# A three-layer graph attention block: products, scores, exponentials and residuals put in another order, and the turn of the normed tokens behind down product 6

## The chip, the cores and the metric

The kernel runs on one core of a Trainium2 chip. The metric is the device time of one execution in microseconds, lower is better. A core has five engines with a queue each: TensorE (PE: matrix products and transposes, results in PSUM), VectorE (DVE), ScalarE (ACT: activations), GpSimd (POOL), and SyncE (SP), which here issues all DMAs. The queues run in order and meet through semaphores.

## The reference

Sixteen graphs of 512 tokens with 256 features, and an adjacency matrix each. All is in fp32.

```python
h = maximum(layernorm(x), 0)
for l in range(3):                                    # the L0 network
    scores = si[:, :, None] + sj[:, None, :] + attn_b[l]   # si, sj = h @ attn_w[l, :256], h @ attn_w[l, 256:]
    attn = softmax(where(adj or diagonal, leaky_0.2(scores), -inf), axis=-1)
    y = layernorm(h + attn @ h) * g1[l] + beta1[l]
    h = layernorm(y + gelu(y @ W1[l] + b1[l]) @ W2[l] + b2[l]) * g2[l] + beta2[l]
x = x + h
h = maximum(layernorm(x), 0)
Wh = h @ W                                            # the L1 network, W is 256 x 256
e = where(adj > 0, leaky_0.2(Wh @ a1 + (Wh @ a2).T), -9e15)
x = x + leaky_0.2(softmax(e, axis=1) @ Wh)
```

## The kernel before

**Pairs and slots.** The graphs are worked in eight pairs. For a pair there are six slots, one per layer and side (a side is one graph of the pair). Slot n does the feed-forward of layer l for the graph of its side, and beside it the attention of the other graph (step n + 1), which will have its feed-forward in the next slot. `Slot` (line 241) says what else falls into a slot. With k = 2 x layer + side, and not in the first pair: in k = 0 and k = 2 a graph of the pair before enters the L1 network (`s.final`: normalise, turn, project, bounded scores), and one slot later, in k = 1 and k = 3, its output is made (`s.late`: exponentials, column scale, product, leaky residual, store). In k = 4 and 5 the next pair's input and masks are prepared (`s.prepare`). Where the attention step is one of layer 0 (`soon`; k = 5 and k = 0) the scores come from the input and are there early.

**Precision.** The feed-forward products are made in three fp32r passes: high x high, high x low, low x high. So h (transposed, normed tokens) and the gelu outputs each exist as a high part and a low part. `h_split` (line 687, ScalarE) makes of the turned tokens in PSUM `h_hi[k]` and `h_full[k]` for k = 0, 1; `h_rest` (line 946, VectorE) makes `h_lo[k]` from `h_full[k]`. `gelu` (line 695, ScalarE) makes the full value `g_full` and the high part `gelu_hi`; `gelu_rest` makes `gelu_lo`, on VectorE for f = 1, 3, 4 and on GpSimd for f = 0, 2, 5, 6, 7. `gelu_hi` and `gelu_lo` are rings of three.

**TensorE's order in a slot.** `up_first` (both first output blocks of W1), `up` 2 and 3, `down` 0 and 1, then `up` and `down` alternating, with the other graph's work between: `scores_row` (s_j as a row for the neighbour maximum), `bound_rows`, `attend_out` (the attention product), and at the end of the slot `turn_tokens` (transposes of `normed` into `ps_t`), `down` 6 and `down` 7. Each `down` adds into `acc`; the first one, line 473, also adds the residual by a transposing product (`residual`, line 466).

**VectorE's order in a slot.** `ff_norm` of the graph before (line 963): statistics of `acc` (L970), variance, high part of gelu 0 (L956), dot products for the next scores (L983), shifts (L992), gelu_lo 1 (L960), then from the dots s_i and s_j (L1006, L1011, L1015); `neighbour_max` (line 875), gelu_lo 3 and 4, `bounded_scores`, `attention_sum`, `attention_norm` (L942), `prepare_masks` where due, and `h_rest`; in slots with `s.final`, `final_bounded` (line 1045) with `h_rest` in it. GpSimd makes the inverse roots (L1236), gelu_lo (L1270), the scaled layer input (L1246, L1250), half of the masked scores (L1276) and the low part of the weights in the first pair (L1291). An order written out by hand, no planner, sets all of this.

The tail of a slot on TensorE before:

```python
                up(n, layer, 7)
                down(n, side, layer, 5)
                pe.wait_ge(q_ready.sem, q_ready.at(n + 1))
                turn_tokens(normed, ln1_apply, h_tr, n + 1, ps_t)
                down(n, side, layer, 6)
                if s.prepare is not None:
                    mask_transposes(s.prepare, side, free)
                down(n, side, layer, 7)
```

On GpSimd, `gelu_rest(n, 7)` stands behind a wait for all four chunks of `ln1_apply` (lines 1330 to 1333). On ScalarE, a change between exponentials and gelus is a table load (ACT_TABLE_LOAD).

## Time and profile before

| | |
|---|---|
| median of 3 runs | 2128.69 us (2128.28 to 2129.1) |
| the profiled execution | 2126.3 us, span 2124.5 us |
| busy: TensorE products, weight loads | 1907.7 us (90%), 1618.6 (76%) |
| busy: VectorE, ScalarE, GpSimd | 1637.2 (77%), 1254.6 (59%), 880.9 (41%) |
| mean granted TensorE clock | 0.969 of full |
| DMA | 52.34 MB, mean 25 GB/s |

The profile is of one execution; times in its rows count from the start of the span. The end of a TensorE product is modelled, and products overlap, so two products that follow each other start closer than their durations. The granted clock has two levels here, 1.2 and 2.4 GHz; a mean of 0.96 in a stretch says that part of it ran at the lower one.

### The profile page before, as it was taken

What the parts mean: (1) busy time and instruction counts of PE and PEld (TensorE: products, weight loads), DVE (VectorE), ACT (ScalarE), POOL (GpSimd) and SP (SyncE); (2) the same over time, 40 slices, a digit from 0 to 9 for tenths busy, and PEclk for the clock granted to TensorE, in tenths of its full rate; (3) what the DMA queues carried; (4) which work ended last, traced back from release to release, by engine and by line L of the source; (5) the groups of instructions that cost most, each with busy time, mean ns of one, the idle gap of its engine ahead of it and who ended that gap; (6) DMA issues with size and microseconds to landing.
All of it is one profiled execution on the core that took longest, in us unless ns stands there. A gap on an engine that the chain in (4) does not pass through costs nothing.

```text
span 2124.5 us, 30899 instructions
## 1 busy us (share of the span) xinstructions
PE 1907.7 (90%) x11009; PEld 1618.6 (76%) x11009; DVE 1637.2 (77%) x4980; ACT 1254.6 (59%) x1948; POOL 880.9 (41%) x703
## 2 busy tenths in 40 slices
PE   3888899998998989999899998999899898999995
PEld 2777777787787877778778777777787787777874
DVE  6778887688777887878878688777886678876765
ACT  3555566566666565665665655656556666565662
POOL 2345453335433444333534344433443334533351
PEclk9999999999999999999999999999999999999998
DMA  4000100010000110001100001000100011000100
GB/s 159 21 30 21 60 11 21 1 40 31 11 21 1 40 41 1 21 1 41 40 1 21 11 35 35 1 21 21 50 11 15 7 39 32 11 11 1 31 1 20
DMA packets 40626, 52.34 MB, mean 25 GB/s; under 512 B 2926, under 2 KB 30872, under 8 KB 40472
## 3 DMA queue, kind: packets, MB, share of 16 engines
q1 hardware_dynamic: 40472, 50.37, 7.3%
q8 instruction: 87, 1.43, 0.3%
q14 instruction: 67, 0.55, 0.1%
HBM read 41.97 MB, written 8.39 MB: 24 GB/s over the span
## 4 chain that ended last, share of the span: by engine, by line
PE 42%; DVE 35%; POOL 9%; ACT 8%; issue 7%; DMA 0%; DVEq 0%; POOLq 0%; ACTq 0%
PE acc L423 11%; PE acc L489 9%; PE ps_u L462 7%; PE acc L526 5%; DVE probs L910 4%; POOL columns L1236 4%; PE acc L508 3%; PE ps_t L386 2%; POOL probs L1276 2%; DVE junk L983 2%; DVE probs L1049 2%; DVE columns L992 2%; DVE junk L881 2%; DVE probs L1053 2%; DVE stats L970 2%
## 5 line engine op out<-in xcount | busy, mean ns | idle before, releaser
L489 PE MATMUL acc<-w_hi,gelu_hi 128*128 128x256 f32 x1536 | 475.7, 310 | 0.0
L702 ACT ACTIVATE g_full<-ps_u,vec_all 128x512 f32<-128x512 f32 x384 | 259.1, 687 | 348.8 <-PE ps_u L462 186.6
L1270 POOL TENSOR_TENSOR gelu_lo<-g_full,gelu_hi 128x512 fp32r<-128x512 f32 x240 | 312.9, 1308 | 320.9 <-ACT gelu_hi L710 260.6
L489 PE MATMUL acc<-w_lo,gelu_hi 128*128 128x256 f32 x1536 | 437.7, 285 | 0.0
L489 PE MATMUL acc<-w_hi,gelu_lo 128*128 128x256 f32 x1536 | 437.5, 285 | 0.0
L423 PE MATMUL acc<-x_nat,probs 128*128 128x257 f32 x1536 | 374.8, 393 | 34.1 <-ACT probs L677 22.8
L423 PEld LDWEIGHTS acc<-x_nat,probs 128*128 128x128 f32 x1536 | 279.4, 191 | 127.2 <-ACT probs L677 42.9
L1236 POOL TENSOR_TENSOR columns<-columns 128x4 f32<-128x4 f32 x128 | 136.0, 1063 | 533.2 <-DVE columns L842 533.2
L489 PEld LDWEIGHTS acc<-w_hi,gelu_hi 128*128 128x128 f32 x1536 | 298.7, 194 | 4.9
L489 PEld LDWEIGHTS acc<-w_lo,gelu_hi 128*128 128x128 f32 x1536 | 298.5, 194 | 5.1
L489 PEld LDWEIGHTS acc<-w_hi,gelu_lo 128*128 128x128 f32 x1536 | 295.9, 193 | 0.0
L462 PE MATMUL ps_u<-h_hi,w_hi 128*128 128x512 f32 x576 | 244.4, 424 | 32.9 <-ACT g_full L702 26.3
L1276 POOL TENSOR_TENSOR probs<-probs,mask_t 128x512 f32<-128x512 f32 x96 | 130.2, 1359 | 339.8 <-DVE probs L910 335.2
L462 PE MATMUL ps_u<-h_hi,w_lo 128*128 128x512 f32 x576 | 234.0, 406 | 0.0
L462 PE MATMUL ps_u<-h_lo,w_hi 128*128 128x512 f32 x576 | 233.9, 406 | 0.0
L710 ACT ACTIVATE gelu_hi<-ps_u,vec_all 128x512 fp32r<-128x512 f32 x336 | 230.5, 686 | 0.0
L910 DVE SCALAR_TENSOR_TENSOR probs<-ps_t,columns,low_sb 128x512 f32<-128x512 f32 x192 | 135.0, 745 | 99.4 <-ACT low_sb L672 94.3
L462 PEld LDWEIGHTS ps_u<-h_hi,w_hi 128*128 128x128 f32 x576 | 112.5, 195 | 70.3 <-issue 40.3
L677 ACT ACTIVATE probs<-probs,columns 128x512 f32<-128x512 f32 x192 | 129.7, 718 | 46.5 <-POOL probs L1276 46.4
L526 PE MATMUL acc<-wh,probs 128*128 128x256 f32 x512 | 120.5, 390 | 14.2 <-DVE wh L1085 14.2
L462 PEld LDWEIGHTS ps_u<-h_hi,w_lo 128*128 128x128 f32 x576 | 112.8, 196 | 26.5
L462 PEld LDWEIGHTS ps_u<-h_lo,w_hi 128*128 128x128 f32 x576 | 113.2, 197 | 15.7
(129 smaller groups left out, 3703.3 us busy)
## 6 DMA issues: line engine op xcount, KB each, us to landing
adj_in<-adj_dram SPq DMA_DIRECT2D x64, 256.0 KB, 2.7
x_nat<-x_dram SPq DMA_DIRECT2D x16, 512.0 KB, 5.2
x_res<-x_dram SPq DMA_DIRECT2D x16, 512.0 KB, 4.2
out_dram<-x_res SPq DMA_DIRECT2D x64, 128.0 KB, 1.7
x_res<-L_gnn_W_dram SPq DMA_DIRECT2D x5, 1024.0 KB, 5.6
mask_g<-L_gnn_W_dram SPq DMA_DIRECT2D x1, 1024.0 KB, 12.3
attn_row<-L_gnn_attn_w_dram SPq DMA_DIRECT2D x1, 512.0 KB
g_row<-L_gnn_g_dram SPq DMA_DIRECT2D x1, 384.0 KB
```

Source lines behind the costliest of these rows:

```text
L423: last = pe.matmul(acc[side][c % 2][:, 0:D + 1], probs[:, j, c * P:(c + 1) * P], x_nat[:, side, j, :], start=(j == 0), stop=(j == NC - 1))
L462: last = pe.matmul(ps_u[f % 2][:, :], w[:, layer, k, lhs], h[:, k, :], start=(i == 0), stop=(i == len(terms) - 1))
L489: last = pe.matmul(acc[side][c // 2][:, cols:cols + D], h[:, r, tok], w[:, layer, f, :], start=False, stop=(f == FC - 1 and i == 2), skip_ ...
L508: last = pe.matmul(banks[c % 2][:, 0:D + 2], h_last[:, k, c * P:(c + 1) * P], w_last[:, k, :], start=(k == 0), stop=(k == KC - 1))
L526: last = pe.matmul(banks[c % 2][:, 0:D], probs[:, j, c * P:(c + 1) * P], wh[:, j, 0:D], start=(j == 0), stop=(j == NC - 1))
L677: act.activation(probs[:, j, :], probs[:, j, :], ACT.Exp, bias=s_j2[:, j:j + 1]).then_inc(p_ready.sem, 1)
L702: full = act.activation(g_full[:, f % 2, :], ps_u[f % 2][:, :], ACT.Gelu, bias=b1_col[:, layer, f:f + 1])
L710: act.activation(gelu_hi[:, f % RING, :], ps_u[f % 2][:, :], ACT.Gelu, bias=b1_col[:, layer, f:f + 1]).then_inc(gelu_done.sem, 1)
L910: dve.scalar_tensor_tensor(out=probs[:, j, :], in0=ps_t[1][:, :], scalar=s_j8[:, j:j + 1], in1=low_sb[:, :], op0=ALU.add, op1=ALU.max).the ...
L1236: pool.tensor_tensor(to[:, :], var_eps[:, :], minus_half[:, :], ALU.pow).then_inc(done.sem, 1)
L1270: pool.tensor_tensor(gelu_lo[:, f % RING, :], g_full[:, f % 2, :], gelu_hi[:, f % RING, :].bitcast(F32), ALU.subtract).then_inc(lo_done[0] ...
L1276: pool.tensor_tensor(probs[:, j, :], probs[:, j, :], mask_t[:, side, j, :], ALU.add).then_inc(q_masked[0].sem, 1)
```

## The change

It touches the order of work on all four compute engines, and the making of the scores:

- **Turn.** `down` 6 is issued before the turn of the normed tokens, not behind it.
- **h.** `h_split` makes `h_hi[0]`, `h_hi[1]`, then `h_full[0]`, `h_full[1]`. In `final_bounded`, `h_rest` stands after the second greatest value (j == 1), not behind the loop.
- **Scores.** The mean of each attention vector is taken off the vector in the setup of the first pair (8 setup steps per layer for 6), so that the dot products need no correction by the token's mean; both constants are summed into one, which `neighbour_max` adds to s_i. Three waits and four instructions behind the dots become one multiplication. The scaling of s_j moves behind the row chain, with a semaphore (`sj_scaled`) that `bounded_scores` waits for.
- **Late slots** (k = 1, 3). `final_exps` of chunks 0 and 1 moves from the end of the slot before to behind gelu 1; gelu 2 and its low part move behind `ff_apply` and `layer_input`; both `final_scale` move behind the scores; `final_out` of chunks 0 and 1 and `scores_row` move in front of `up` 4.
- **Residual.** Where the slot is not `soon`, `residual` of chunk 0 is issued in front of `up` 2.
- **Others.** gelu 6 before `input_apply` and `keep_mask` on ScalarE; gelu_lo 5 and 6 before `residual_shift` on GpSimd; `final_mask` of k = 5 behind `neighbour_max`.

```diff
@@ down, start_of, slot (TensorE)
-                        residual(n, side, c)
+                        if c not in turned:
+                            residual(n, side, c)
...
-                if s.attend and s.layer_a == 0 and not s.begins:
+                soon = s.attend and s.layer_a == 0 and not s.begins
+                if soon:
                     scores_row(n + 1)
+                else:
+                    residual(n, side, 0)
...
                 down(n, side, layer, 1)
-                if s.attend and s.late is None and (s.layer_a > 0 or s.begins):
+                if s.late is not None:
+                    final_out(s.late[0], acc[s.other], (0, 1), n - 1)
+                if s.attend and (s.layer_a > 0 or s.begins):
                     scores_row(n + 1)
                 up(n, layer, 4)
...
-                if s.late is not None:
-                    final_out(s.late[0], free, (0, 1), n - 1)
-                if s.late is not None:
-                    scores_row(n + 1)
                     final_out(s.late[0], free, (2, 3))
...
                 down(n, side, layer, 5)
+                down(n, side, layer, 6)
 
                 pe.wait_ge(q_ready.sem, q_ready.at(n + 1))
                 turn_tokens(normed, ln1_apply, h_tr, n + 1, ps_t)
-                down(n, side, layer, 6)
@@ h_split and the slot (ScalarE)
                                    bias=beta1_col[:, layer, k:k + 1], scale=g1_col[:, layer, k:k + 1]).then_inc(hi_ready.sem, 1)
+                for k in range(KC):
                     act.activation(h_full[:, k, :], ps_t[k][:, :], ACT.Identity, bias=both_col[:, layer, k:k + 1],
...
-                    gelu(n, layer, 2)
+                    if s.late is None:
+                        gelu(n, layer, 2)
+                    else:
+                        final_exps(s.late[0], (0, 1))
...
                         ff_apply(n - 1, other, 1)
+                    if s.late is not None:
+                        gelu(n, layer, 2)
...
                     gelu(n, layer, 5)
+                    gelu(n, layer, 6)
...
-                    gelu(n, layer, 6)
...
-                    if s.final is not None:
-                        final_exps(s.final[0], (0, 1))
@@ neighbour_max, ff_norm, final_bounded (VectorE)
-                dve.tensor_scalar(s_j8[:, :], s_j, 1.0 - SLOPE, None, ALU.mult)
-                dve.tensor_scalar(s_j2[:, :], s_j, SLOPE, None, ALU.mult)
+                if layer > 0:
+                    dve.tensor_scalar(s_i, s_i, bias_col[:, 0, layer:layer + 1], None, ALU.add)
                 dve.wait_ge(sj_bc.sem, sj_bc.at(n))
...
+                dve.tensor_scalar(s_j8[:, :], s_j, 1.0 - SLOPE, None, ALU.mult)
+                dve.tensor_scalar(s_j2[:, :], s_j, SLOPE, None, ALU.mult).then_inc(sj_scaled.sem, 1)
...
-                if late is not None:
-                    final_scale(late, 0)
...
-                if late is not None:
-                    final_scale(late, 1)
...
-                    for t in (1, 0):
-                        last = dve.scalar_tensor_tensor(out=raw_dots[:, t, :], in0=mean[:, :],
-                                                        scalar=minus_sum[:, t, layer:layer + 1],
-                                                        in1=raw_dots[:, t, :], op0=ALU.mult, op1=ALU.add)
...
-                    dve.tensor_tensor(raw_dots[:, :, :], raw_dots[:, :, :],
+                    dve.tensor_tensor(s_both[:, :, :], raw_dots[:, :, :],
                                       rstd[:, :].rearrange("p (o c) -> p o c", o=1).broadcast_to([P, 2, NC]),
-                                      ALU.mult).then_inc(dots_ready.sem, 1)
-                    dve.wait_ge(dots_ready.sem, dots_ready.at(turn, 2))
-                    dve.tensor_tensor(s_both[:, :, :], raw_dots[:, :, :],
-                                      bias_col[:, :, layer:layer + 1].broadcast_to([P, 2, NC]),
-                                      ALU.add).then_inc(s_ready.sem, 1)
+                                      ALU.mult).then_inc(s_ready.sem, 1)
                     dve.wait_ge(s_ready.sem, s_ready.at(step_next))
+                if late is not None:
+                    final_scale(late, 0)
+                    final_scale(late, 1)
...
-                if step is not None:
-                    h_rest(*step)
+                    if step is not None and j == 1:
+                        h_rest(*step)
@@ the slot (VectorE and GpSimd)
-                    if s.side == 1 and s.layer == LAST:
-                        final_mask(pair * 2 + 1, 1)
-                    neighbour_max(n + 1, other)
+                    neighbour_max(n + 1, other, s.layer_a)
...
                         if s.prepare is not None and s.side == 1:
+                            final_mask(pair * 2 + 1, 1)
                             prepare_masks(s.prepare, 1, (0,))
...
-                    gelu_rest(n, 2)
+                    if s.late is None:
+                        gelu_rest(n, 2)
...
+                    if s.late is not None:
+                        gelu_rest(n, 2)
...
+                    gelu_rest(n, 5)
+                    gelu_rest(n, 6)
                     if s.layer == LAST:
                         residual_shift(pair, s.side)
-                    gelu_rest(n, 5)
-                    gelu_rest(n, 6)
```

## Rows read from the trace of the kernel before

**Rows 1.** The page, section 1: busy time (share of the span) x instructions.
```profile
PE 1907.7 (90%) x11009; PEld 1618.6 (76%) x11009; DVE 1637.2 (77%) x4980; ACT 1254.6 (59%) x1948; POOL 880.9 (41%) x703
```

**Rows 2.** Windows: stretch, length; busy us (instructions) per engine; clock; DMA; GB/s.
```profile
52.84:301.14 248.30, 218.49 (x1257) 186.21 (x1257) 201.27 (x572) 140.12 (x205) 117.64 (x84) 0.95 0.10 30
852.63:896.37 43.74, 41.28 (x238) 34.79 (x237) 33.92 (x114) 27.90 (x43) 17.10 (x14) 1.00 0.08 25
685.03:729.79 44.76, 42.59 (x238) 36.06 (x237) 35.73 (x116) 27.90 (x43) 16.33 (x13) 0.96 0.14 48
896.37:940.44 44.07, 40.59 (x234) 34.50 (x233) 31.11 (x90) 26.79 (x43) 15.95 (x13) 0.96 0.00 1
474.47:515.09 40.62, 35.00 (x222) 29.98 (x221) 35.33 (x109) 24.52 (x39) 19.66 (x16) 1.00 0.08 26
984.23:1027.70 43.47, 37.83 (x223) 32.91 (x221) 36.60 (x115) 25.31 (x40) 19.63 (x16) 0.92 0.11 35
1027.70:1066.75 39.05, 36.10 (x222) 31.68 (x221) 34.76 (x102) 23.07 (x38) 20.21 (x16) 0.96 0.05 17
```

**Rows 3.** Waits of TensorE: us in total, times, longest us.
```profile
PE ps_t L386 <- DVE s_both L1015: 34.7, 18, 2.0
PE ps_t L432 <- DVE normed L942: 27.8, 12, 3.1
PE ps_t L386 <- DVE columns L892: 21.5, 8, 3.3
```

**Rows 4.** Timeline, turn to next slot (1 to 2): start, us, instruction, [idle before].
```profile
892.65 1.03 PE L432 MATMUL ps_t<-ident,normed 128*128 128x128 f32 x8
...
895.62 0.78 ACT L692 ACTIVATE h_last<-ps_t,vec_all 128x512 f32<-128x512 f32 x1
...
896.43 0.75 DVE L949 SCALAR_TENSOR_TENSOR h_lo<-h_last,vec_all,h_hi 128x512 fp32r<-128x512 f32 x1 [0.51 <-ACT h_last L692]
```

**Rows 5.** Timeline, head of slot 2, which starts at 896.37.
```profile
897.22 1.43 DVE L970 BATCH_NORM_STATS2 stats<-acc 128x6 f32<-128x256 f32 x4
...
904.48 1.45 DVE L1006 SCALAR_TENSOR_TENSOR raw_dots<-columns,vec_all,raw_dots 128x4 f32<-128x4 f32 x2
...
907.19 1.18 DVE L1015 TENSOR_TENSOR s_both<-raw_dots,vec_all 128x8 f32<-128x8 f32 x1
...
904.51 1.28 POOL L1246 TENSOR_TENSOR x_nat<-normed,g_row 128x512 f32<-128x512 f32 x1
...
908.42 0.93 PE L386 MATMUL ps_t<-ident,s_both 128*128 128x128 f32 x4 [1.95 <-DVE s_both L1015]
```

**Rows 6.** Timeline, head of slot 1 (late), which starts at 852.63.
```profile
852.68 1.28 ACT L736 ACT_TABLE_LOAD   x1
...
853.90 1.40 DVE L949 SCALAR_TENSOR_TENSOR h_lo<-h_last,vec_all,h_hi 128x512 fp32r<-128x512 f32 x2
...
856.20 1.42 DVE L970 BATCH_NORM_STATS2 stats<-acc 128x6 f32<-128x256 f32 x4
...
868.31 0.17 DVE L1015 TENSOR_TENSOR s_both<-raw_dots,vec_all 128x8 f32<-128x8 f32 x1
...
857.64 0.47 PE L462 MATMUL ps_u<-h_hi,w_hi 128*128 128x512 f32 x1 [1.32 <-ACT g_full L702]
...
859.61 1.29 POOL L1270 TENSOR_TENSOR gelu_lo<-g_full,gelu_hi 128x512 fp32r<-128x512 f32 x1
```

**Rows 7.** Timeline, end of slot 4, which ends at 1027.70.
```profile
1017.98 0.16 DVE L842 SCALAR_TENSOR_TENSOR columns<-columns 128x4 f32<-128x4 f32 x1
...
1019.84 1.02 POOL L1236 TENSOR_TENSOR columns<-columns 128x4 f32<-128x4 f32 x1
...
1022.35 1.51 POOL L1270 TENSOR_TENSOR gelu_lo<-g_full,gelu_hi 128x512 fp32r<-128x512 f32 x1 [1.50 <-DVE normed L942]
...
1021.45 1.73 PE L432 MATMUL ps_t<-ident,normed 128*128 128x128 f32 x7 [2.53 <-DVE normed L942]
```

**Rows 8.** Timeline, bound rows of slot 5, which starts at 1027.70.
```profile
1041.65 1.67 PE L386 MATMUL ps_t<-ident,columns 128*128 128x128 f32 x7 [2.57 <-DVE columns L892]
```

29 lines of the change are left out of this document (15 added, 14 removed).

## The prediction

> **What bounds the kernel now.** I read the page's first two sections, then the windows view, then the waits of TensorE, then the timeline. TensorE is busy 90% of the span [rows 1], so the change, which takes no product away, can win at most the idle tenth and what the slow clock adds. I call the eight products of one feed-forward f = 0 to 7, and I number the six slots of a pair 0 to 5 (2 x layer + side); a slot starts with the first product of `up_first`. The windows view [rows 2] shows the first pair (248.30 us) and slots of later pairs, and where the clock falls: in one late slot of 44.76 us the mean is 0.96, in another of 43.74 it is 1.00; it is 0.96 in slots 2 and 5, 1.00 and 0.92 in two slots 4. The waits of TensorE [rows 3] name three large causes: the scores of the next layer (34.7 us, 18 times), the normed tokens of the turn (27.8 us, 12 times) and the bound rows (21.5 us, 8 times). These are waits for VectorE's chain, so the question of each part is what it does to VectorE's time within the slot.
>
> **Part 1, the turn behind down product 6, high parts first.** Today a turn starts at 892.65, ScalarE's last full part ends at 896.39, VectorE's last low part at 897.18, and the next slot starts at 896.37 [rows 4]. Turn and two down products fill the 3.72 us between; the turn, 1.03 with its overlap into the next product, fills some 0.85 of them, and half of the rest is 1.43 for one product. Moved in front, product 6 fills a wait of the turn where there is one. Where there is none (slots 0 to 3 of later pairs), the turn starts 1.43 later in a slot of the same length, so `h_rest` ends and the next `ff_norm` starts 1.43 later in the next slot: 2.3 after its start in place of 0.85 [rows 5]. TensorE itself hardly waits there: both high parts are now ready 1.5 after the first can be made, product 7 covers that, and the low parts come at most 0.3 late.
> What that delays: down product 0 waits for `gelu_lo` 0, which ends 4.7 us after `ff_norm` starts (856.20 to 860.90 in slot 1 [rows 6]). So in slots 2 and 4 product 0 starts at 6.95 of the slot, about 0.75 later than today; the wait is short and I expect no fall of the clock from it.
> In late slots (1 and 3) it is worse. `h_rest` now stands after the second of the bounded rows and waits there for ScalarE's third activation of the new order; the last bounded rows and maxima come behind it: 0.9 us from the end of `h_rest` (855.30) to `ff_norm` (856.20) today [rows 6], and the 1.3 that stood before it, together 2.2. `ff_norm` starts 4.5 into the slot, today 3.57 [rows 6], and `gelu_lo` 0 is done at 9.25 instead of 8.27. Taking the exponentials off ScalarE's head (a table load of 1.28 and two exponentials, for which up product 2 waits 1.32 [rows 6]) wins 0.9 at up product 2, but this is lost again, as product 0 waits for VectorE: one wait of 2.9 us. Behind a wait of 2.57 in slot 5 seven transposes take 1.67 us [rows 8], where eight of the turn take 1.03 [rows 4]: the clock has fallen. A mean of 0.96 over 44.07 us is 3.4 us at half pace, up to 1.7 lost; six of the 14 late slots lose 1.0 already (44.76 against 43.74 [rows 2]). So I add 0.85 on average for the clock. Fourteen late slots times (0.95 + 0.85) = **+25 us**; bounds +0.5 and +3.3 each, so +7 and +46.
>
> **Part 2, fewer steps to the scores.** Two L1006, one L1011 and one L1015 become one multiplication. In slot 2 they run from 904.48 to 908.37, and TensorE waits 1.95 us for them [rows 5]. L1015 takes 1.18 there and 0.17 in slot 1 [rows 6]; L1006 ends at 905.93, just behind POOL's first instruction of `layer_input` (904.51 to 905.79) [rows 5], and L1011 and L1015 behind the next two. So I count one such stall for the one instruction that is left. With `ff_norm` 1.43 later, and `gelu` 2 on ScalarE later by the same, the last shift ends at 9.65 of the slot, and the multiplication at 9.8 (not held) or 11.0 (held); TensorE arrives at 10.6. I take 11.0, today 12.05: 1.05 won.
> The Trainium skill, page "SBUF — State Buffer", section "Who interferes with whom", says that a DVE instruction with two SBUF inputs contends with a GpSimd instruction that reads SBUF, and that whoever comes first holds the pair for the whole instruction. By that rule the one multiplication left is held up and the gain is 1.05, by its absence 1.45; the trace agrees (1.18 against 0.17).
> In slot 2 everything behind is ScalarE's: final apply, two gelus, `final_h`, which set when `project` starts. So the whole win is what moves `final_shift`, 1.0 to 1.2: seven slots, **-7.7 us** (bounds -5 and -17). The scaling of s_j behind the row chain and the bias in front of it are two small instructions against two; the scaling is hidden by VectorE's wait for the bound rows. The early `residual` of token chunk 0, 0.22 us, falls into the 0.4 us that up product 2 waits; in slots 2 to 4 the later wait gives it back, so nothing.
>
> **Part 3, slot 4.** Here both things meet. The scores come 1.05 earlier and the slow stretch behind them (up to 1.5 us, in two of six such slots with both) goes. At the end, POOL makes the inverse root only at 1019.84 although the variance is ready at 1018.14, because gelu_lo 6 waited for ScalarE, which made `keep_mask` first; the turn waits 2.53 us [rows 7]. In the new order gelus 5 and 6 precede the input and the mask, so the root starts at once (1.7 earlier), and product 6 (1.43) covers what is left. What comes next: product 7 waits for `gelu_lo` 7, which POOL makes only behind the four normed chunks (1022.35 to 1023.86, 1.6 behind the chunks' end [rows 7]), and the mask's transposes wait for chunk 3 of `prepare_masks`, 1.9 behind it. That is a wait of 0.6. Counted through: slot 4 takes 37.5 us; the six of today take between 40.62 and 43.47, mean 42.2 [rows 2]. Six times -4.7 = **-28 us** (bounds -2.0 and -5.5 each).
>
> **Part 4, slots 5 and 0.** Slot 5 starts nearer to VectorE's mask, scores and `h_rest` of the slot before, so `ff_norm` starts at 2.9 of the slot, today 1.08: VectorE is the bound of slot 5 (34.76 of 39.05 us busy [rows 2]). `final_mask`, 1.13 us, leaves its place before the row chain, and the held scaling too; the bound rows then come at 13.2 to 14.4, today 13.95 [rows 8]. But mask and scaling are only put behind, before `bounded_scores`, and POOL's `layer_input` is still at work then; TensorE's attention product of chunks 2 and 3 waits for VectorE. I get +0.3 to +2.6, take +1.5: six slots **+9 us**. Slot 0 is 0.3 later each, seven times: **+2 us**. The last pair's slot 4 has no masks (-1.1), and the last slot runs on VectorE's chain (+1.2): nothing.
>
> **Part 5, the first pair.** It has no late slots and its turns wait most (3.1 us at the longest [rows 3]). Here the turn does not move later, so VectorE keeps its place in the slot and the scores are ready before TensorE comes: slots 1 and 2 win 2.0 us of wait and 1.5 of clock each, slot 3 some 2.0. But at the turn only about 0.3 is won, since product 7 then waits for `gelu_lo` 7 (product 6 used to cover that). With 5 from slot 4, 1.3 lost in slot 5, and four more setup steps in shadow: -0.3 -4.1 -4.0 -3.3 -5 +1.3 = **-15 us** (bounds -8 and -18).
>
> **Sum.** 25 - 7.7 - 28 + 9 + 2 - 15 = -15 us on the profiled execution of 2126.3 us (span 2124.5). The median of the runs is 2128.69, which is 2.4 above it; I carry the difference to the median: 2128.7 - 15 = 2114.
>
> **The rivals.**
> (a) The late slots pay more. One mechanism, in front of down product 0 of slots 1 and 3: `final_scale` now lies behind the scores, so if the multiplication is held twice and the clock falls every time, product 1 ends early only to have `final_out` wait for the second half of wh. Then each costs 3.3 instead of 1.8: +21, 2135 us. It decides from 2.9 us each; at that the whole gain is gone. For it: 2.9 us of wait is longer than any today in these slots; against it: half-pace products leave VectorE the time.
> (b) The covered waits come back. The turn's wait in slot 4 is replaced by that for `gelu_lo` 7 and the masks, and slot 5 gives the rest back, so that slot 4 wins 2.0, not 4.7: +16, 2130 us. For it: rows 7 show POOL's gelu_lo 7 1.6 behind the tokens, and product 6 is no longer there to hide it. Against it: the root's 1.7 do not depend on it.
> (c) The late slots lose nothing: ScalarE, rid of two table loads per late slot, or a `gelu_lo` 0 earlier than I count, keeps product 0 at 8.3. Then -25: 2089 us. For it: up product 2 waits for ScalarE alone today.
> That the change does not do what it says would need that the turn is not behind the products at all in effect: where the tokens are late by more than 1.43 (only the first pair), most of it remains; this is in (b).
>
> **Chances and range.** Forecast 0.47 (2099 to 2124), (a) 0.18, (b) 0.15, (c) 0.20. The range 2088 to 2135 takes in the centres of all, and leaves out the outer half of (a) and of (c). A measurement here tells 0.2% (4.3 us) from no change. Faster: nearly all of the forecast, all of (c) and a third of (b), 0.69; within 0.2%: most of (b) and the edges, 0.13; slower: (a), 0.18.
>
> **What would show it.** In the changed trace: no wait of the turn over 0.6 us in slot 4, and a root (L1236) directly behind the variance; `ff_norm` 2.3 us into slots 2 and 4 and 4.5 into slots 1 and 3; in these one wait of about 2.9 us for `gelu_lo` in front of the first down product, with half-pace products behind it; scores waits under 0.6 us in slots 2 and 4; the first pair near 233 us. The prediction is wrong if slots 1 and 3 keep their 43.7 us, or if slot 4 stays above 40.

## The result and the profile after

The changed kernel is slower by half a per cent, where a gain of 15 us was forecast.

| | before | after |
|---|---|---|
| median of the runs, us | 2128.69 (five runs, 2126.22 to 2129.10) | 2137.79 (five runs, 2135.63 to 2139.53) |
| ratio after to before | | 1.0046, 95% interval 1.0031 to 1.0060 |
| profiled execution, us | 2126.30 | 2137.79 |
| its span, mean granted clock | 2124.5, 0.969 | 2136.0, 0.981 |

The span grew by 11.5 us although the granted clock rose from 0.969 to 0.981. The clock has two levels, 2.4 and 1.2 GHz, so the means say that 0.062 x 2124.5, some 132 us, ran at the lower one before, and 81 us after. The loss is time in which TensorE waits, and it is more than the 11.5 us: the part of the span in which it is not busy grew from 2124.5 - 1907.7 = 216.8 us to 2136.0 - 1903.6 = 232.4, by 15.6.

The page of after, section 1 (the counterpart of [rows 1]):

```profile
PE 1903.6 (89%) x11009; PEld 1594.1 (75%) x11009; DVE 1628.4 (76%) x4920; ACT 1218.9 (57%) x1920; POOL 881.1 (41%) x703
```

VectorE runs 60 instructions fewer and is busy only 9 us less. Windows of after: the first pair, a slot 1, a slot 2, a slot 3, a slot 4 and a slot 5, with the columns of [rows 2]:

```profile
53.08:286.26 233.18, 213.78 (x1257) 180.44 (x1257) 187.75 (x568) 138.19 (x202) 117.71 (x84) 0.97 0.10 32
845.48:893.41 47.93, 43.07 (x239) 36.49 (x237) 36.10 (x111) 25.42 (x41) 17.08 (x14) 0.96 0.07 23
893.41:936.16 42.75, 39.52 (x235) 33.21 (x233) 29.37 (x88) 26.73 (x44) 16.04 (x13) 1.00 0.00 1
936.16:984.07 47.91, 41.52 (x238) 34.93 (x237) 37.91 (x113) 25.43 (x41) 16.30 (x13) 1.00 0.14 45
984.07:1021.33 37.26, 35.10 (x223) 29.78 (x221) 33.06 (x106) 25.58 (x40) 19.74 (x16) 1.00 0.07 21
1021.33:1062.84 41.51, 37.28 (x223) 30.68 (x222) 36.64 (x110) 22.73 (x38) 20.03 (x16) 0.96 0.11 34
```

In these windows everything is shorter than before except slots 1, 3 and 5, and both late slots take 47.9 us whether the clock is 0.96 or 1.00 in them: what bounds them there is not TensorE's pace. The waits of TensorE in after name what does (the counterpart of [rows 3]):

```profile
PE acc L490 <- POOL gelu_lo L1270: 47.4, 33, 2.7
PE acc L527 <- DVE wh L1084: 42.5, 23, 7.5
...
PE acc L396 <- DVE mask_nat L861: 17.0, 12, 5.3
...
PE ps_t L386 <- DVE columns L899: 3.6, 2, 3.4
PE ps_t L432 <- DVE normed L952: 2.9, 3, 2.1
```

The three causes of [rows 3] are gone or small: there is no row for the next layer's scores (now L1011), 2.9 us are left at the normed tokens of the turn where it was 27.8, and 3.6 at the bound rows where it was 21.5. In their place are two: the first low part of gelu (L1270), as forecast, and **wh**, which `final_scale` (L1084) scales for the output product of the final layer. No term of the forecast's sum priced the second; only rival (a) named it. Here is the head of the late slot that starts at 936.16, first VectorE, then POOL, then TensorE's waits (the counterpart of [rows 6]):

```profile
940.77 1.42 DVE L980 BATCH_NORM_STATS2 stats<-acc 128x6 f32<-128x256 f32 x4
...
947.82 0.15 DVE L1011 TENSOR_TENSOR s_both<-raw_dots,columns 128x8 f32<-128x8 f32 x1
948.01 0.17 DVE L1081 RECIPROCAL columns<-columns 128x2 f32<-128x2 f32 x1
948.21 2.46 DVE L1084 TENSOR_SCALAR wh<-wh,columns 128x256 f32<-128x256 f32 x2
950.59 0.15 DVE L1081 RECIPROCAL columns<-columns 128x2 f32<-128x2 f32 x1
950.78 2.33 DVE L1084 TENSOR_SCALAR wh<-wh,columns 128x256 f32<-128x256 f32 x2
```

```profile
946.59 1.30 POOL L1246 TENSOR_TENSOR x_nat<-normed,g_row 128x512 f32<-128x512 f32 x1 [1.15 <-ACT normed L686]
947.96 1.29 POOL L1250 TENSOR_TENSOR x_nat<-x_nat,beta_row 128x512 f32<-128x512 f32 x1
949.21 1.31 POOL L1246 TENSOR_TENSOR x_nat<-normed,g_row 128x512 f32<-128x512 f32 x1
950.60 1.09 POOL L1250 TENSOR_TENSOR x_nat<-x_nat,beta_row 128x512 f32<-128x512 f32 x1
951.64 1.31 POOL L1270 TENSOR_TENSOR gelu_lo<-g_full,gelu_hi 128x512 fp32r<-128x512 f32 x1
```

```profile
945.49 0.39 PE L490 MATMUL acc<-w_hi,gelu_hi 128*128 128x256 f32 x1 [2.74 <-POOL gelu_lo L1270]
...
950.82 1.10 PE L527 MATMUL acc<-wh,probs 128*128 128x256 f32 x4 [1.54 <-DVE wh L1084]
953.16 2.86 PE L527 MATMUL acc<-wh,probs 128*128 128x256 f32 x12 [1.25 <-DVE wh L1084]
```

Up to product 0 the slot runs as forecast (`ff_norm` 4.61 into the slot, a wait of 2.74). Then two scalings take 2.46 us and the next two 2.33, and they follow POOL's instructions in step: the first pair ends at 950.67 and the second at 953.11, POOL's instructions end at 949.25, 950.52, 951.69 and 952.95. TensorE waits 1.54 and 1.25 for them. In the late slot that starts at 845.48, where the clock's mean is 0.96, only one of these two waits is there, of 1.24.

The end of slot 4 (the counterpart of [rows 7]), VectorE's last step of the variance, POOL's root, TensorE's turn and the wait behind it:

```profile
1014.95 0.17 DVE L849 SCALAR_TENSOR_TENSOR columns<-columns 128x4 f32<-128x4 f32 x1
...
1015.26 1.02 POOL L1236 TENSOR_TENSOR columns<-columns 128x4 f32<-128x4 f32 x1 [1.12 <-DVE columns L849]
...
1017.16 1.04 PE L432 MATMUL ps_t<-ident,normed 128*128 128x128 f32 x8
...
1019.63 0.40 PE L396 MATMUL acc<-ident_b,mask_nat 128*128 128x128 bf16 x4 [0.77 <-DVE mask_nat L861]
```

The root starts 0.14 us after the end of the variance, the turn waits for nothing, and what is late next is the mask, by 0.77.

**Where the time went.** Mean length of a slot, from its first up product to the next slot's, over the pairs behind the first (slot 4 and 5 without the last pair's), and the same for four kernels of the next section that bear on the reading:

| us | before | after | turn_back | both | scores_only | sg_resid |
|---|---|---|---|---|---|---|
| slot 1 (7) | 44.03 | 47.91 | 47.03 | 45.35 | 43.85 | 43.85 |
| slot 3 (7) | 44.34 | 47.91 | 47.03 | 45.34 | 43.81 | 43.81 |
| slot 2 (7) | 44.00 | 42.74 | 41.24 | 41.30 | 41.19 | 41.18 |
| slot 4 (6) | 42.20 | 37.28 | 36.68 | 36.65 | 39.02 | 36.65 |
| slot 5 (6) | 39.26 | 41.17 | 40.56 | 40.58 | 39.44 | 39.64 |
| first pair | 248.3 | 233.2 | 236.4 | 234.2 | 235.5 | 231.9 |

After against before, times the counts: slots 1 and 3 +27.1 and +25.0, slot 2 -8.8, slot 4 -29.5, slot 5 +11.5, slot 0 -0.1, first pair -15.1, the last pair's slot 4 and last slot +1.2 together. The sum is +11.3, the span's own difference 11.5. How far a single figure can be trusted shows in the first pair, which has no late slot: after, scale_accum and scale_back run the same instructions in it and take 233.2, 231.2 and 231.4.

### The profile page after: what moved, and what is told of

It reads as the page before. It is cut to its first block, busy times and chain, and to the rows that moved or that the text cites. A ratio compares the mean times of both kernels' runs of the same rounds, so it can differ in the third digit from the quotient of the medians.

```text
span 2136.0 us, 30833 instructions
## 1 busy us (share of the span) xinstructions
PE 1903.6 (89%) x11009; PEld 1594.1 (75%) x11009; DVE 1628.4 (76%) x4920; ACT 1218.9 (57%) x1920; POOL 881.1 (41%) x703
## 4 chain that ended last, share of the span: by engine, by line
PE 40%; DVE 39%; ACT 8%; POOL 7%; issue 6%; DMA 0%; DVEq 0%; POOLq 0%; ACTq 0%
PE acc L423 12%; PE acc L490 10%; PE ps_u L462 6%; PE acc L527 5%; DVE probs L920 5%; POOL columns L1236 3%; DVE wh L1084 3%; DVE stats L980 3%; PE acc L509 3%; DVE h_lo L959 3%; DVE junk L991 3%; POOL probs L1276 2%; DVE junk L888 2%; DVE stats L834 2%; DVE columns L1000 2%
## 5 line engine op out<-in xcount | busy, mean ns | idle before, releaser
L490 PE MATMUL acc<-w_hi,gelu_hi 128*128 128x256 f32 x1536 | 473.1, 308 | 55.1 <-POOL gelu_lo L1270 47.4
L423 PE MATMUL acc<-x_nat,probs 128*128 128x257 f32 x1536 | 386.7, 400 | 52.0 <-ACT probs L680 26.8
L1270 POOL TENSOR_TENSOR gelu_lo<-g_full,gelu_hi 128x512 fp32r<-128x512 f32 x240 | 309.9, 1299 | 265.1 <-ACT gelu_hi L714 205.8
L490 PEld LDWEIGHTS acc<-w_hi,gelu_hi 128*128 128x128 f32 x1536 | 294.3, 192 | 77.0 <-POOL gelu_lo L1270 61.8
L462 PE MATMUL ps_u<-h_hi,w_hi 128*128 128x512 f32 x576 | 239.7, 416 | 9.9 <-ACT wh L731 6.7
L462 PE MATMUL ps_u<-h_hi,w_lo 128*128 128x512 f32 x576 | 227.4, 395 | 0.0
L462 PE MATMUL ps_u<-h_lo,w_hi 128*128 128x512 f32 x576 | 227.0, 394 | 0.0
L527 PE MATMUL acc<-wh,probs 128*128 128x256 f32 x512 | 125.1, 395 | 42.5 <-DVE wh L1084 42.5
L527 PEld LDWEIGHTS acc<-wh,probs 128*128 128x128 f32 x512 | 97.7, 195 | 65.0 <-DVE wh L1084 37.7
L693 ACT ACTIVATE h_hi<-ps_t,vec_all 128x512 fp32r<-128x512 f32 x96 | 69.5, 775 | 113.6 <-PE ps_t L432 113.6
```

Source lines behind the costliest of these rows:

```text
L423: last = pe.matmul(acc[side][c % 2][:, 0:D + 1], probs[:, j, c * P:(c + 1) * P], x_nat[:, side, j, :], start=(j == 0), stop=(j == NC - 1))
L462: last = pe.matmul(ps_u[f % 2][:, :], w[:, layer, k, lhs], h[:, k, :], start=(i == 0), stop=(i == len(terms) - 1))
L490: last = pe.matmul(acc[side][c // 2][:, cols:cols + D], h[:, r, tok], w[:, layer, f, :], start=False, stop=(f == FC - 1 and i == 2), skip_ ...
L527: last = pe.matmul(banks[c % 2][:, 0:D], probs[:, j, c * P:(c + 1) * P], wh[:, j, 0:D], start=(j == 0), stop=(j == NC - 1))
L693: act.activation(h_hi[:, k, :], ps_t[k][:, :], ACT.Identity, bias=beta1_col[:, layer, k:k + 1], scale=g1_col[:, layer, k:k + 1]).then_inc( ...
L1270: pool.tensor_tensor(gelu_lo[:, f % RING, :], g_full[:, f % 2, :], gelu_hi[:, f % RING, :].bitcast(F32), ALU.subtract).then_inc(lo_done[0] ...
```

## The experiments

Two theories stood at the start. The first: the late slots lose by `final_scale`, whose instructions now run beside POOL's `layer_input` and are held by it. The second: they lose by the wait for `gelu_lo` 0, which the moved turn makes, and by the slow clock behind it. The ratios below are to the kernel before, run beside each kernel; medians are in us.

### scale_accum: the scaling in a form that writes its accumulator too

Edit to after. 1 - SLOPE is folded into the reciprocal by a small instruction of its own:

```
+ dve.tensor_scalar(col_r[:, cols], col_r[:, cols], 1.0 - SLOPE, None, ALU.mult)
...
- last = dve.tensor_scalar(wh[:, c, 0:D], wh[:, c, 0:D], col_r[:, c:c + 1], 1.0 - SLOPE, ALU.mult, ALU.mult)
+ last = dve.tensor_scalar(wh[:, c, 0:D], wh[:, c, 0:D], col_r[:, c:c + 1], 0.0, ALU.mult, ALU.add,
+                          accum_out=col_max[:, c:c + 1])
```

> The changed kernel, with the four scalings of wh in final_scale in the form that also writes an accumulator (the factor 0.8 is put into the reciprocal by one more small instruction per half). Place and order stay. In the changed kernel's trace two of them take 2.46 and 2.33 us in a late slot, where before they took 0.62, and they end when POOL's layer_input does. Theory 1 (they are held by POOL because of their form): 0.5 us each whatever POOL does, second half of wh ready near 14.5 of the slot in place of 16.95, late slots 47.9 to about 45.5, 14 times -2.4: about 2104 us. Theory 2 (the late place in VectorE's order costs, the holding does not matter or hits this form too): late slots stay at 47.9, 2138 us or a little more. The Trainium skill, page 'SBUF — State Buffer', section 'Who interferes with whom', says of tensor_scalar that the form which also writes out its accumulator cannot take the shared ports; by that rule theory 1 holds.

Measured: 2116.59, ratio 0.9955 (0.9940 to 0.9970), 21 less than after. VectorE in the late slot that starts at 927.73, and POOL beside it:

```profile
939.76 1.05 DVE L1083 TENSOR_SCALAR columns<-columns 128x2 f32<-128x2 f32 x1
940.84 0.48 DVE L1086 TENSOR_SCALAR_CACHE_REDUCE wh<-wh,columns 128x256 f32<-128x256 f32 x1
941.25 0.08 DVE L1086 DVE_READ_ACCUMULATOR wh<-wh,columns 128x1 f32 x1
941.25 0.48 DVE L1086 TENSOR_SCALAR_CACHE_REDUCE wh<-wh,columns 128x256 f32<-128x256 f32 x1
```

```profile
940.74 1.28 POOL L1249 TENSOR_TENSOR x_nat<-normed,g_row 128x512 f32<-128x512 f32 x1
```

Inside one instruction of POOL two scalings now end within 0.9 us; the second half of wh is ready 15.2 us into the slot instead of 16.95, and TensorE no longer waits for it. But slots 3 take 46.2 us and slots 1 47.4; to give the 34 us that theory 1 expected, each would have to take 47.9 - 2.4 = 45.5. Windows of one of each (starts 837.55 and 927.73):

```profile
837.55:884.94 47.39, 43.80 (x238) 37.74 (x237) 34.34 (x117) 25.38 (x41) 16.99 (x14) 0.93 0.07 23
927.73:973.96 46.23, 42.62 (x239) 36.43 (x238) 36.13 (x119) 25.40 (x42) 16.23 (x13) 0.96 0.14 46
```

The wait for `gelu_lo` 0 is still 2.73 and 2.74, and by the means of these windows the clock is at its lower level for some 6.6 us in the first slot (2 x 0.07 x 47.39) and 3.7 in the second. In after a slow stretch was covered by VectorE's lateness; now it is the limit. So the hold is real. Of the 21 us, 15.4 are gained in the fourteen late slots (7 x 0.52 + 7 x 1.68), where theory 1 expected 34; the rest is slot 5 (4.5) and the first pair (2.0), which the edit doesn't touch. What is missing in the late slots lies behind a second limit, the wait for `gelu_lo` 0 with the slow clock.

### scale_back: the scaling at its old places

```
+                if late is not None:
+                    final_scale(late, 0)   # behind gelu_high
...
+                if late is not None:
+                    final_scale(late, 1)   # behind half(1)
```

> The changed kernel with the two final_scale at their places of before: half 0 behind the high part of gelu 0, half 1 behind the second shift and in front of the scores. Theory 1 (holding by POOL): half 0 now falls where POOL is idle or makes the root, only half 1 meets layer_input; second half of wh ready near 15, late slots near 46: 14 times -1.9, about 2112 us. Theory 2 (what costs is that VectorE comes to the late slot 1.0 later, by the turn): down product 0 stays at 9.3 and half 0 waits for the exponentials up to 0.4, so late slots stay above 47: 2130 to 2140 us.

Measured: 2122.78, ratio 0.9984 (0.9974 to 0.9993), 15 less than after, between the two theories; slots 1 and 3 take 47.2. Two of the four scalings in the slot that starts at 930.62, what POOL did at that moment, and TensorE's wait:

```profile
938.38 1.69 DVE L1085 TENSOR_SCALAR wh<-wh,columns 128x256 f32<-128x256 f32 x2
...
944.32 2.50 DVE L1085 TENSOR_SCALAR wh<-wh,columns 128x256 f32<-128x256 f32 x2
```

```profile
938.65 1.26 POOL L1271 TENSOR_TENSOR gelu_lo<-g_full,gelu_hi 128x512 fp32r<-128x512 f32 x1
...
944.13 1.27 POOL L1251 TENSOR_TENSOR x_nat<-x_nat,beta_row 128x512 f32<-128x512 f32 x1
945.36 1.31 POOL L1247 TENSOR_TENSOR x_nat<-normed,g_row 128x512 f32<-128x512 f32 x1
```

The old place in the order is not the old place beside POOL. The first two scalings stand 7.76 us into the slot instead of 6.25 (858.88), since `ff_norm` is 1.06 later [rows 6], and the second of them meets `gelu_lo` 0. The other two stand at 13.70, as before (13.61), but `layer_input` now comes ahead of gelu_lo 2 on POOL and is there at that moment. Over the whole execution the groups by line of before and of scale_back say it in one number (min, median and longest of one instruction, ns):

```profile
L1085 DVE TENSOR_SCALAR wh<-wh,columns x64: 347/352/356, 349.3 to 2112.5; 128x256 f32<-128x256 f32 x64
```

```profile
L1085 DVE TENSOR_SCALAR wh<-wh,columns x64: 346/1244/1426, 334.0 to 2108.7; 128x256 f32<-128x256 f32 x64
```

Before, none of 64 was held; here, in VectorE's old order, 42 are, three of the four in every late slot. The hold comes from the meeting, and two other edits of the change bring it about as well: the turn's move for the first two scalings (sg_turn below shows it, with POOL's old order) and, as the rows above read, POOL's new order for the last two.

### turn_back: product 6 behind the turn again

```
  down(n, side, layer, 5)
- down(n, side, layer, 6)
  ...
  turn_tokens(normed, ln1_apply, h_tr, n + 1, ps_t)
+ down(n, side, layer, 6)
```

> The changed kernel with down product 6 behind the turn again, everything else as changed. Theory 1 (the turn delays ff_norm by 1.4 in slots 2, 4 and by 1.0 in 1, 3, 5): down product 0 of a late slot at 8.3 in place of 9.3, late slots 46.9 (the held scalings stay), slot 5 about 1 shorter, slot 4 about 1 longer by its turn's wait, slot 2 about 1 shorter, first pair some 2 to 4 longer: 14 + 6 + 7 - 6 - 3 = 18 us less, 2120. Theory 2 (the turn is neutral, all loss is in the late slots' new order): 2136 to 2142 us.

Measured: 2105.80, ratio 0.9900 (0.9886 to 0.9915), 32 less than after, where theory 1 had 18. Every kind of slot in the table gains, slot 2 most (42.74 to 41.24); only the first pair loses 3.2. **Slot 4 takes 36.68 without the moved turn against 37.28 with it**: its gain is not the turn's. The late slots gain 0.9 each and stop there. The wait for `gelu_lo` is 2.12 now, but the hold is as it was (L1084: 2.47 and 2.33 us for two), and TensorE waits 1.25 for wh. Again one of two limits was taken away and the other one stayed.

### turn_only: the turn's move and ScalarE's order alone, in the kernel before

```
+ down(n, side, layer, 6)
  pe.wait_ge(q_ready.sem, q_ready.at(n + 1))
  turn_tokens(normed, ln1_apply, h_tr, n + 1, ps_t)
- down(n, side, layer, 6)
...
+ for k in range(KC):
      act.activation(h_full[:, k, :], ...)
```

> The kernel before with only product 6 in front of the turn and both high parts made before the full parts. Theory 1 (turn delays VectorE): slots 1 and 3 +1.2 to +1.8, slots 2 and 4 +1.4 at the scores, slot 5 +1.4, against -1.4 at the turn of slot 4 and -0.3 in the first pair: +17 to +25, +10, +8, +8, -8: 2160 us, range 2150 to 2170. Theory 2 (turn is neutral): within 4 of 2128.7.

Measured: 2180.52, ratio 1.0251 (1.0236 to 1.0266), 52 more than before, beyond the range that was expected. Its waits of TensorE beside [rows 3]:

```profile
PE ps_u L462 <- ACT g_full L703: 45.8, 33, 2.7
PE ps_t L386 <- DVE s_both L1016: 44.9, 18, 2.6
```

The wait for the scores grows from 34.7 to 44.9 us and that at up product 2 reaches 2.7 in the late slots, where it was 1.32 [rows 6]. Slots 1 and 3 take 46.2 and 45.4, slots 2 and 4 some 1.4 and 1.0 more than before. The turn's own wait falls from 27.8 to 4.4 us, as it was meant to, and everything that hangs on the later turn costs more than that.

### both: turn back and accumulating form together

The two edits turn_back and scale_accum.

> Two of the earlier edits at once on the changed kernel: product 6 behind the turn again, and the scalings of wh in the accumulating form. Alone they took 32 us and 21 us off. Theory 1 (two separate mechanisms on one chain of VectorE: the turn sets when ff_norm starts in the late slot, the hold by POOL lengthens the scaling behind it): they add up, 2137.8 - 32 - 21 and some 8 more, since product 0 now comes 1.0 earlier and the slow stretches get rarer: 2078 us, 2072 to 2087. Theory 2 (the slow clock behind the wait of product 0 is what sets the late slots, each edit only uncovers it): 2095 or more.

Measured: 2086.76, ratio 0.9809 (0.9793 to 0.9826). The late slots take 45.35: 2.56 less than after, where the two edits alone took off 0.88 and 1.10 (mean of slots 1 and 3 in scale_accum: 46.81). That is more than the sum. Alone, each edit left one limit in its place: scale_accum the wait of 2.74 with the slow clock behind it, turn_back the wait for wh. TensorE in the late slot that starts at 917.39:

```profile
925.83 0.39 PE L490 MATMUL acc<-w_hi,gelu_hi 128*128 128x256 f32 x1 [2.13 <-POOL gelu_lo L1273]
...
930.69 3.99 PE L527 MATMUL acc<-wh,probs 128*128 128x256 f32 x16 [1.10 <-DVE wh L1086]
```

Still 1.2 above before. `ff_norm` stands 3.72 into the slot, near the 3.57 of before [rows 6], and product 0 starts at 8.44, near the 8.32 of before. So the wait for `gelu_lo` 0 only takes the place of the one that up product 2 had (1.32 [rows 6]). What is late now is wh, by 1.10, and the small scaling of the reciprocal in front of it is held here (1.07).

### late_back: the whole order of the late slots as before, on turn_back

`final_exps(0, 1)` at the end of the slot before, gelu 2 early, `final_scale` and `final_out` at their old places; ScalarE's new order of the high parts and `h_rest` behind the second bounded row stay.

```
+ if s.final is not None:
+     final_exps(s.final[0], (0, 1))   # behind h_split
...
+ final_out(s.late[0], free, (0, 1), n - 1)   # behind up product 4
```

> The changed kernel with product 6 behind the turn and with the late slots in their old order (exponentials 0 and 1 at the end of the slot before, gelu 2 and its low part early, final_scale at its old places, output product behind up 4). What stays of the change: the cheaper scores, the early residual, gelu 6 before mask and input, h in the new order, h_rest earlier. Theory 1 (the new late order is itself a loss of about 3 us a slot, whatever the turn does): late slots 43.5 to 44.0 in place of 47.0: 2105.8 - 14 x 3.2 = 2061 us. Theory 2 (the new late order is sound and only the turn spoilt it): 2100 to 2110.

Measured: 2069.79, ratio 0.9729 (0.9715 to 0.9744), 17 less than both and 36 less than turn_back, which has the late slots' new order and is otherwise the same. So that order is a loss by itself, also without the moved turn. Slots 1 and 3 take 45.33 and 43.96: in both kinds up product 2 waits 2.5 us, and the windows of one of each show a mean clock of 0.96 and 1.00. None of its scalings is held, in the plain form (columns as above):

```profile
L1083 DVE TENSOR_SCALAR wh<-wh,columns x64: 346/352/357, 336.1 to 2057.2; 128x256 f32<-128x256 f32 x64
```

The change without the turn's move and the late order is 59 us faster than before.

### g6_only: gelus 5 and 6 ahead of input and mask, in the kernel before

```
  gelu(n, layer, 5)
+ gelu(n, layer, 6)
  ...
- gelu(n, layer, 6)
```

and on POOL `gelu_rest` 5 and 6 ahead of `residual_shift`.

> The kernel before with one thing: gelu 6 before input_apply and keep_mask on ScalarE, gelu_lo 5 and 6 before residual_shift on POOL. My step was: in slot 4 the root follows the variance at once, 1.7 earlier, the turn's wait falls from 2.5 to about 0.9 and the slow stretch behind it mostly goes. Theory 1 (this order is what wins slot 4's end): seven slots 4 times 2 to 2.8: 2127.3 - 16 = 2111 us. Theory 2 (it was product 6 in front of the turn that covered the wait): 2122 to 2127.

Measured: 2105.58, ratio 0.9893 (0.9878 to 0.9907). Slot 4 takes 39.29 instead of 42.20; TensorE's wait for the normed tokens falls from 27.8 us [rows 3] to this:

```profile
PE ps_t L432 <- DVE normed L942: 15.0, 12, 1.8
```

So slot 4's end is won by the order of two gelus, with the turn where it was.

### scores_only: the centred attention vectors and the single multiplication, in the kernel before

```
- (two L1006, L1011, L1015 and their waits)
+ dve.tensor_tensor(s_both[:, :, :], raw_dots[:, :, :], rstd..., ALU.mult)
```

with the centring in `attention_vectors` and the bias and scaling in `neighbour_max`, as in the change.

> The kernel before with only the scores part: centred attention vectors, one multiplication behind the dots, bias in neighbour_max, scaling of s_j behind the row chain. Theory 1 (the scores' wait in slots 2 and 4 goes nearly whole when ff_norm is not late): slot 2 -1.5 to -2, slot 4 -2.3, slot 5 -1 (held scaling), slots 1 to 3 of the first pair -3 each: about -12, -16, -7, -9: 2083 us, 2078 to 2095. Theory 2 (POOL holds the one instruction that is left as long as the four): slots 2 and 4 -1 each, 2110.

Measured: 2070.46, ratio 0.9729 (0.9715 to 0.9744): **58 us from this part alone**, more than the forecast gave to the whole change and below the 2078 to 2095 that was expected here. The groups by line of before (L1011, L1015) and of scores_only (L1008), ns of one:

```profile
L1011 DVE TENSOR_TENSOR raw_dots<-raw_dots,columns x32: 1120/1176/1192, 107.1 to 2019.5; 128x8 f32<-128x8 f32 x32
...
L1015 DVE TENSOR_TENSOR s_both<-raw_dots,vec_all x32: 166/1182/1192, 108.3 to 2020.7; 128x8 f32<-128x8 f32 x32
```

```profile
L1008 DVE TENSOR_TENSOR s_both<-raw_dots,columns x32: 152/155/164, 105.3 to 1962.5; 128x8 f32<-128x8 f32 x32
```

Of the chain's four instructions L1011 was held for an instruction of POOL in all 32 cases, L1015 and one L1006 in 18 of them (not in the late slots); of the one instruction that is left, none of 32 is. TensorE doesn't wait for these scores at all: slots 2 and 4 become 2.8 and 3.2 us shorter, the first pair 12.8, the late slots 0.2 and 0.5. The wait itself was 34.7 us [rows 3]. The mean clock rose from 0.969 to 0.988, so that some 50 us ran at the lower level instead of 132; that slow stretches went with the waits is most of the other 23 us, as an estimate from these means.

### scores_g6: both of these

> The kernel before with the scores part and with gelu 6 before input and mask, nothing else of the change. Alone they took 58 and 23 us off. Theory 1 (they act at different places of the slots and add up, less what both count of the same slow stretches): 2128.3 - 58 - 17 = 2054 us, 2046 to 2060. Theory 2 (the one hides the other in slot 4): 2065 to 2070.

Measured: 2061.28, ratio 0.9680 (0.9664 to 0.9697); slot 4 takes 36.94. The time is a little above the expected 2046 to 2060: against scores_only slots 1 and 3 are 0.30 and 0.15 longer, slot 5 0.26 and the first pair 0.7. Three of the fourteen late slots take 44.8 us here, the others 43.8 to 44.1.

### sg_turn: the turn's move and ScalarE's order on top of scores_g6

> The kernel of scores_g6 with product 6 in front of the turn and both high parts first: the two edits that the change is named for, on a base where all else that helps is kept and the late slots are the old ones. Theory 1 (ff_norm starts 1.4 later in each slot and nothing hides it): slots 1 and 3 +2.1 and +1.3 as on the kernel before, slot 2 +1.5, slot 4 +0.6, slot 5 +0.7, first pair -2: +40 us over scores_g6, about 2094. Theory 2 (with the cheap scores there is slack for the 1.4): +5 at the most.

Measured: 2106.13, ratio 0.9908 (0.9888 to 0.9928): **45 us lost by the two edits**, as turn_only said. (The profiled execution took 2114.4, 8 us above the median, so its slots are read a little too long.) TensorE in the late slot that starts at 929.13:

```profile
935.55 0.47 PE L462 MATMUL ps_u<-h_hi,w_hi 128*128 128x512 f32 x1 [2.73 <-ACT g_full L703]
```

The wait at up product 2 is 1.4 us longer than in scores_g6, with a slow stretch behind it; slots 1 and 3 take 47.1 and 46.2 instead of 44.15 and 43.96, slot 2 42.76 instead of 41.19. Which of the two edits does it can be read from ScalarE. Its four activations on the turned tokens end 1.45 us into this slot, in scores_g6 at 0.03; they start 1.42 later and take 2.79 in both. So it is product 6 in front of the turn that delays the exponentials and the gelus behind them; ScalarE's order of the four doesn't. The scalings say how much of the hold is the turn's:

```profile
L1079 DVE TENSOR_SCALAR wh<-wh,columns x64: 341/352/1460, 334.0 to 2101.8; 128x256 f32<-128x256 f32 x64
```

14 of 64 are held, the first in every late slot; the others aren't. TensorE doesn't wait for wh in these slots. With the late order as before, the moved turn costs by ScalarE's lateness, not by the hold.

### sg_hrest: the low parts of h behind the second bounded row, on top of scores_g6

```
-                if step is not None:
-                    h_rest(*step)
+                    if step is not None and j == 1:
+                        h_rest(*step)
```

> The kernel of scores_g6 with h_rest behind the second greatest value in final_bounded, nothing else. Late slots of late_back (which has this, 45.3 and 44.0) are longer than those of scores_only (43.8 both). Theory 1 (h_rest early makes VectorE wait for ScalarE's h_full, and the last maxima, the exponentials 0 and 1 and gelu 0 behind them come later): late slots +0.2 to +1.5, 14 times 0.8: +11 us over scores_g6. Theory 2 (low parts early help TensorE at the start of late slots): -3 to 0.

Measured: 2080.71, ratio 0.9777 (0.9763 to 0.9792): 19 lost, where 11 was the larger of the expectations. VectorE and ScalarE in the late slot that starts at 917.28, and what TensorE does:

```profile
917.24 1.40 DVE L952 SCALAR_TENSOR_TENSOR h_lo<-h_last,vec_all,h_hi 128x512 fp32r<-128x512 f32 x2
...
919.95 0.34 DVE L1051 TENSOR_SCALAR columns<-columns 128x1 f32<-128x1 f32 x2
```

```profile
920.13 0.72 ACT L736 ACTIVATE probs<-probs,columns 128x512 f32<-128x512 f32 x1 [0.70 <-DVE columns L1051]
```

```profile
923.09 0.77 PE L462 MATMUL ps_u<-h_hi,w_hi 128*128 128x512 f32 x1 [2.86 <-ACT g_full L702]
```

`h_rest` in front of the maxima makes an exponential wait 0.70 us, and the gelus stand behind the exponentials on ScalarE: TensorE waits 2.86 at up product 2 and the clock falls behind it. This is what remained in late_back, which kept this edit (2069.8 against 2053.2 of the next kernel). late_back also kept ScalarE's order of the high parts and the new place of `final_mask`. If the edits add, scores_g6 with `h_rest` (+19.4) and the residual (-8.1) would take 2072.6, and late_back takes 2069.8, so these two are worth little together; that they add is an assumption.

### sg_resid: the residual of token chunk 0 ahead of up product 2, on top of scores_g6

```
+ else:
+     residual(n, side, 0)
  up(n, layer, 2)
```

> The kernel of scores_g6 with the residual of token chunk 0 in front of up product 2 in slots that are not soon. Theory 1 (0.2 us of work go into the wait of 0.4 in slots 1 to 4, and with the scores no longer late nothing takes it back): 31 slots times 0.2 = 6 us less than scores_g6. Theory 2 (the next wait, for gelu_lo or for the scores, gives it back, as I predicted for the changed kernel): no difference, within 2.

Measured: 2053.15, ratio 0.9649 (0.9635 to 0.9664), the fastest of all: 3.5% under before, 4.0% under after. The gain of 8 us against scores_g6 isn't spread as theory 1 had it. Slot 2 is unchanged (41.19 and 41.18) and the shortest late slots are too (43.80 in both), so there the next wait gives it back, as the prediction had it. What is shorter is slot 4 (36.94 to 36.65), the first pair (236.2 to 231.9, of which 2 can be chance by the spread told above), and the late slots of 44.8 us, of which there were three and are none.

**The call taken apart.** By ratios, times 2128.7, each kernel against the one before it in this row: scores -57.7, gelu order -10.4, turn's move and ScalarE's order +48.5, the rest (the late slots' order, `h_rest`, mask and residual) +29.4. The sum is +9.8, the measured result, as it must be: the terms are differences along one path from before to after. On another path they have other sizes: in the changed kernel the moved product is worth 32 us (turn_back), and the late order 36 once the product is back (late_back).

## Why the prediction was wrong

**Part 1, late slots: the step that failed.** The term was +1.8 per late slot, +25 in all; measured +3.72 (47.91 against 44.19, the mean of both), +52. The 27 us between them are the error of the sum (-15 forecast, +11.5 measured); those of the other parts nearly cancel. Its first half held to 0.2 us: `ff_norm` 4.61 into the slot (forecast 4.5), product 0 at 9.33 (9.25), a wait of 2.74 (2.9). What was wrong is what stands behind product 0. There the sum let the slot go on as in before and added 0.85 for the clock. In truth TensorE waits 1.54 + 1.25 = 2.79 us for wh. Between slots at full clock the loss is 47.91 - 43.74 = 4.17: product 0 starts 1.01 later (forecast 0.95), the two waits are 2.79, and 0.37 are not traced. The mean loss is smaller, 3.72, because six of the 14 late slots of before already lost 1.0 to the clock. In after the clock costs nothing on top, for in the slots where it falls the wait for VectorE is shorter by as much (47.93 at 0.96 with 1.24 of wait for wh, 47.91 at 1.00 with 2.79).

The wait had not been seen because `final_scale` was carried at its old duration: Part 1 has no term for it. It was counted as a moved instruction, not as one that comes to stand beside another engine's work. Four scalings took 1.24 us in the head of slot 1 of before, at 858.88 and 866.24, the first beside POOL's short root (858.51 to 859.63) and the second in the gap before 866.99; moved beneath `layer_input` they take 4.79. Part 2 had the rule in hand, from the 1.18 of L1015 against 0.17 [rows 5, 6], and used it for the scores' small vectors alone. scale_accum shows that it is the hold: the same work in another form, beside the same instructions of POOL, takes 0.9 for two, TensorE's wait for wh is gone from the late slots, and they gain 15 us. scale_back shows that the new place on VectorE isn't needed for it: the moved turn and POOL's new order are enough.

**Rival (a)** named the place, the wait of `final_out` for the second half of wh, and gave 2135, near the measured 2137.8. Its cause was another one: a multiplication held twice and a clock that falls each time. The multiplication was held in none of 32 cases, and the clock wasn't the limit. It was right in its arithmetic (from 2.9 us per late slot the gain is gone) and too cheap in its chance, 0.18, because its condition was one of my own making instead of a duration to be read: how long is this instruction when POOL is at work?

**Part 2** forecast -1.1 per slot 2; measured -1.26, -8.8 in all. The two halves of it were wrong and cancelled. The multiplication was expected to be held and end at 11.0, with TensorE there at 10.6; it isn't held in any slot (why is open, see the last section), and nothing waits. Alone, the part takes 2.8 us off slot 2 (scores_only). Of this the moved turn gives 1.5 back (42.74 against 41.24 in turn_back), where Part 1 had 0.75, covered, for it.

**Part 3** forecast 37.5 for slot 4, -28; measured 37.28, -29.5. The root at once, the wait of 0.6 for the mask (0.77): as read. But the part that the text gave to product 6 is not there. With the product behind the turn the slot is 0.6 shorter. What wins is the order of the gelus (g6_only) and the scores. So this total is right with one of its causes wrong, which is luck.

**Part 4** forecast +9 for slot 5; measured +11.5 (41.17 against 39.26). As read, the wait moves from the bound rows (2.6 us per slot before, 0.1 after) to the attention product, which waits 2.1 for VectorE's normed chunks (0.3 before). But this isn't the turn's: with product 6 back, slot 5 still takes 40.56 and has the same wait. Slot 0 +2 forecast, -0.1 measured.

**Part 5** forecast -15; measured -15.1, to 233.2, a figure good to 2 us. Here the moved turn does win: 3.2 us by turn_back, 4.1 by sg_turn (236.2 to 232.1); in turn_only, with the old scores, it wins nothing (248.9 against 248.3). The scores alone give 12.8.

**Rival (b)** did not happen, **rival (c)** neither. Of the signs named in advance, every one came in but for the clock behind product 0, which fell in some slots only. Of the two signs that would refute the forecast, "slots 1 and 3 keep their 43.7" looks the wrong way: nothing was named that would show them longer than forecast, which is what came.

The forecast's larger fault isn't in the sum. It judged the change as a whole and had no term for what each part is worth alone. The moved turn costs 32 us in the changed kernel and, with ScalarE's order, 45 and 52 on the two others; the late order costs 36 once the turn is back. Together they stood in the sum as +25. The scores, -58 alone, stood in it as -7.7 and a share of the first pair's and slot 4's gain. Terms taken inside the combination can be right to 3 us and still hide that one part eats another's gain.

## What to carry to other kernels

When an instruction moves in VectorE's order, or when what stands in front of it comes later, look at what POOL does at the new time and price it both ways; here 0.35 us became 1.2 for each of four, and with VectorE's old order beside POOL's new one three of the four were still held. If the work can't be moved, a form that isn't held is worth an extra small instruction. And a step that fills TensorE's wait at the end of a slot by delaying the hand-over to a busy engine has to be priced at everything that this engine feeds in the next slot: in turn_only it won 23 us of wait at the turn, and the kernel lost 52 all the same. Where two limits stand one behind the other, taking one away shows only part of what it costs, and neither edit alone tells what both would bring (0.88 and 1.10 us per late slot, together 2.56).
